# VectorE divides all 32 heads in one pass and rotates the keys of both batches in one pass

## The reference

```python
x = x + tanh(g_xattn[0]) * L0_xattn(layernorm(x), mask, ctx, Wq, Wk, Wv, Wo, gate)
x = x + tanh(g_ffn[0]) * L0_ffn(layernorm(x), wg, W, b)
x = x + tanh(g_xattn[1]) * L1_xattn(w, u, layernorm(x), ctx)
x = x + tanh(g_ffn[1]) * L1_ffn(layernorm(x), w_gate, w1, w2, w3)

# L0_xattn: 32 heads of 8 columns, rotary q and k
q = q * cos + rotate_half(q) * sin
k = k * cos + rotate_half(k) * sin
w = softmax(q @ k.T / sqrt(8) + mask)
attn = w @ v
a_scores = tanh(gate) * softmax(q @ a_k.T / sqrt(8))   # a_k, a_v from ctx, not rotated
attn = attn + a_scores @ a_v
return attn @ Wo
```

## Time and profile before

| | |
|---|---|
| median of 3 runs | 542.29 us (541.72 to 549.66) |
| the profiled execution | 543.49 us |
| its span in the trace | 541.6 us |
| TensorE busy | 476.9 us, 88% |
| TensorE weight loads | 355.0 us, 66% |
| VectorE busy | 392.6 us, 72% |
| ScalarE busy | 263.7 us, 49% |
| GpSimd busy | 169.7 us, 31% |
| mean granted clock of TensorE | 0.954 |
| loop over tiles | to about 300 us |

### The profile page before, as it was taken

How to read it: one execution, slowest core, us unless ns; L and a number is a source line. 1 busy time by engine, 2 the same in 40 slices (tenths; PEclk the granted TensorE clock), 3 DMA queues, 4 the chain that set the end, 5 groups by cost and what they waited for, 6 DMA issues and landing times. The chain is left out here.

```text
span 541.6 us, 10345 instructions
## 1 busy us (share of the span) xinstructions
PE 476.9 (88%) x3090; PEld 355.0 (66%) x3091; DVE 392.6 (72%) x1042; ACT 263.7 (49%) x562; POOL 169.7 (31%) x228
## 2 busy tenths in 40 slices
PE   4589999999989988988988859877889999999994
PEld 2458678667567576675776636545568788878782
DVE  4856878788897897888987777937676566556640
ACT  2546283374462662743731432511646666666651
POOL 4150204114113123141131143220345556555622
PEclk9888997999999999999998958988999999999997
DMA  7921304004004004022040179553657667767721
GB/s 239 278 42 21 62 3 79 5 23 79 5 21 79 15 10 77 24 38 45 21 80 6 39 301 422 201 159 128 229 146 232 206 204 230 249 208 195 232 27 21
DMA packets 24755, 63.38 MB, mean 117 GB/s; under 512 B 5161, under 2 KB 15281, under 8 KB 21777
## 3 DMA queue, kind: packets, MB, share of 16 engines
q1 hardware_dynamic: 19440, 56.38, 33.9%
q0 software_dynamic: 4416, 6.03, 6.1%
q10 hardware_dynamic: 864, 0.54, 0.3%
HBM read 48.79 MB, written 5.24 MB: 100 GB/s over the span
## 5 line engine op out<-in xcount | busy, mean ns | idle before, releaser
L1901 PE MATMUL bank_o<-w,hT 128*128 (+1 forms) x276 | 70.4, 398 | 1.1 <-DVE hT L1323 0.7
L1337 DVE TENSOR_TENSOR wl<-lw,wh 128x1024 fp32r<-128x1024 f32 (+1 forms) x54 | 60.9, 1129 | 0.3 <-ACT wh L621 0.3
L1901 PEld LDWEIGHTS bank_o<-w,hT 128*128 128x128 f32 (+1 forms) x276 | 50.4, 195 | 15.6 <-issue 10.0
L494 POOL TENSOR_SCALAR rstd<-mv 128x1 f32<-128x1 f32 x32 | 7.2, 225 | 168.4 <-DVE mv L956 168.4
L1028 DVE TENSOR_REDUCE mx<-bank_s 128x8 f32<-128x512 f32 x64 | 43.3, 686 | 14.7 <-PE bank_s L1645 14.2
L621 ACT ACTIVATE wh<-lw 128x1024 fp32r<-128x1024 f32 (+1 forms) x54 | 53.0, 981 | 0.0
L1643 PE MATMUL bank_s<-Kh,Qx 128*128 128x128 f32 x256 | 43.2, 293 | 4.6 <-DVE mx L1028 3.3
L1330 DVE TENSOR_TENSOR hh<-sg,bank_s 128x256 f32<-128x256 f32 x46 | 19.1, 418 | 35.9 <-ACT sg L849 26.8
L1643 PEld LDWEIGHTS bank_s<-Kh,Qx 128*128 128x128 f32 x256 | 37.1, 202 | 7.5 <-DVE mx L1028 4.0
L575 POOL DMA_INDIRECT out_x<-ys,idx_out x18 | 29.0, 1609 | 37.6 <-ACT ys L860 36.8
L662 ACT ACTIVATE Qx<-qs,CN 128x512 fp32r<-128x512 f32 x56 | 35.2, 710 | 5.5 <-DVE qs L1001 5.4
(11 more groups left out here) (346 smaller groups left out, 1157.3 us busy)
## 6 DMA issues: line engine op xcount, KB each, us to landing
lw<-in_w SPq DMA_DIRECT2D x18, 1408.0 KB, 6.5
Q<-Qx SPq DMA_DIRECT2D x16, 512.0 KB
up<-in_w SPq DMA_DIRECT2D x5, 1408.0 KB, 6.9
w<-in_w SPq DMA_DIRECT2D x4, 1536.0 KB, 11.8
Pt<-in_WT SPq DMA_DIRECT2D x1, 1024.0 KB, 11.8
X<-in_x SPq DMA_DIRECT2D x1, 896.0 KB, 8.3
CT<-in_ctxT SPq DMA_DIRECT2D x1, 896.0 KB, 8.7
out_x<-X SPq DMA_DIRECT2D x6, 128.0 KB, 1.7
```

The source lines that it names most:

```text
L1337: dve.tensor_tensor(wl[par][:, :, at:at + k], lw[par][:, :, at:at + k], wh[par][:, :, at:at + k].bitcast(F32), ALU.subtract).then_inc(w_lo, 1)
L1901: ins = pe.matmul(bo[:, 0:HID], hT[0:k, i, :], w2[0:k, bass.ts(e, 1), i, :].rearrange("p o n -> p (o n)"), start=(i == 0), stop=(i == IT - 1))
```

## The change

1. `heads` can do all 32 heads at once. In the loop it is called once per tile, where the first of its two calls stood, between the maxima of units 2 and 3; it waits for all four groups of `Oc` where the first call waited for three. In the last tile's tail the two calls stay.
2. `ao_in` counts one per tile instead of two; ScalarE's and TensorE's waits for it are changed to that.
3. `rotate_ks` rotates both batches' keys with the same four operations on operands twice as wide; it is called where the first `rotate_k` stood, ahead of the third norm's `ln_apply(2, u)`. The second call, behind it, is gone. The set-up of tile 0 still calls `rotate_k` twice.

```diff
@@ -689,7 +689,7 @@
                 if g == 0:
-                    after(act, ao_in, t - 1, 2, 2)
+                    after(act, ao_in, t - 1, 1, 1)
@@ -964,18 +964,23 @@
+            def both(ap):
+                return ap[:, :, :].rearrange("p b n -> p (b n)")
+
             def twice(ap):
-                return ap.rearrange("p (g o d) -> p g o d", g=G, o=1).to_broadcast([P, G, 2, HG * D])
+                n = ap.shape[-1] // (HG * D)
+                return ap.rearrange("p (g o d) -> p g o d", g=n, o=1).to_broadcast([P, n, 2, HG * D])
@@ -994,6 +999,15 @@
+            def rotate_ks(t):
+
+                after(dve, k_in, t, BT, BT)
+                rope(both(kw), C_COSK, C_SINK, both(kt1), both(kt2)).then_inc(rope_step, BT)
+                after(dve, rope_step, t, 1 + BT, 1 + BT)
+                after(dve, kT, t - 1, BT, BT)
+                dve.tensor_tensor(kr[:, :, :, :, :].rearrange("p b g o d -> p (b g) o d"), twice(both(kt1)), twice(both(kt2)),
+                                  ALU.add).then_inc(k_rot, BT)
@@ -1035,12 +1049,12 @@
-            def heads(t, part):
-
-                r = (slice(0, H - HG), slice(H - HG, H))[part]
+            def heads(t, part=None):
+
+                r = slice(0, H) if part is None else (slice(0, H - HG), slice(H - HG, H))[part]
                 n = r.stop - r.start
-                link = Chain(dve, heads_step, t, 6, 3 * part)
-                after(dve, o_in, t, G, (3, 4)[part])
+                link = Chain(dve, heads_step, t, 3, 3 if part == 1 else 0)
+                after(dve, o_in, t, G, 3 if part == 0 else G)
@@ -1395,10 +1409,8 @@
                 if prev:
-                    heads(u, 0)
+                    heads(u)
                 maxima(t, range(3, 4))
-                if prev:
-                    heads(u, 1)
                 maxima(t, range(4, 6))
@@ -1437,11 +1449,10 @@
                 if nxt:
-                    rotate_k(t + 1, 0)
+                    rotate_ks(t + 1)
                 if prev:
                     ln_apply(2, u)
                 if nxt:
-                    rotate_k(t + 1, 1)
                     mask_low(t + 1, 1 - par)
@@ -1709,7 +1720,7 @@
             def turn_heads(t, following, o=bc):
-                after(pe, ao_in, t, 2, 2)
+                after(pe, ao_in, t, 1, 1 if following else 2)
```

More of the change, by code:

```diff
@@ L965, in ln_apply @@
                                   ALU.subtract, ALU.mult).then_inc(ln_done[n], 1)
+            def both(ap):
+                return ap[:, :, :].rearrange("p b n -> p (b n)")
             def twice(ap):
-                return ap.rearrange("p (g o d) -> p g o d", g=G, o=1).to_broadcast([P, G, 2, HG * D])
+                n = ap.shape[-1] // (HG * D)
+                return ap.rearrange("p (g o d) -> p g o d", g=n, o=1).to_broadcast([P, n, 2, HG * D])
             def rope(src, cos, sin, t1, t2):
-                v = src.rearrange("p (h d) -> p h d", h=H)
+                m = src.shape[-1] // D
+                v = src.rearrange("p (h d) -> p h d", h=m)
                 def bc3(c, n):
-                    return c.rearrange("p (o d) -> p o d", o=1).to_broadcast([P, H, n])
-                a = t1.rearrange("p (h d) -> p h d", h=H)
-                z = t2.rearrange("p (h d) -> p h d", h=H)
+                    return c.rearrange("p (o d) -> p o d", o=1).to_broadcast([P, m, n])
+                a = t1.rearrange("p (h d) -> p h d", h=m)
+                z = t2.rearrange("p (h d) -> p h d", h=m)
                 h = D // 2
```

## The result

The changed kernel takes **551.91 us** (median of 4 runs, 550.89 to 562.09) against 542.0 for the kernel before on the same chip (4 runs): **1.018 times as long, 95% interval 1.0153 to 1.0206**. The forecast was 540.0 us in a range of 538.0 to 543.8, so the time lies on the other side and outside. The profiled execution took 552.45 us with a span of 550.6, which is 8.96 us more than the one of before. Ratios and means here leave out the executions that count as slow, more than 1.5% above the fastest of the same kernel, while medians, lowest and highest times hold all of them.

A forecast was written before the change was run, and what follows sets the result against it. The prediction saw TensorE and VectorE both nearly full, so waits between them decide. Heads gain 3.6 us and k's rotation costs 1.3, taking the median of 542.29 to 540.0 us, range 538.0 to 543.8.

The forecast's parts named there:

- Heads: One 1.94 us pass on VectorE brings ao earlier and removes TensorE's waits for it; gain 3.6 us over the loop.
- k: Merged rotation on VectorE takes 2.65 us; h3 starts 1.08 us later, decay scan 0.22 us later per tile, 1.3 us in all.
- Sum: Whole kernel: 3.6 us gained and 1.3 us lost, so 2.3 us less than the median of 542.29 us.
- A: All of VectorE's saving in both merged passes counts: 8.5 us, giving 533.8 us; chance 0.06.
- B: Wide heads pass runs over its price, so its gain is lost and h3's lateness stays: 543.6 us; chance 0.15.
- C: TensorE's 1.3 us idle ahead of h3 lowers its clock, costing 2 us of at most 3: 542.0 us; chance 0.13.
- fuller form: Clock falls between hn and the second norm cost 1.7 us each, six giving 550 us; chance 0.03 for over 545.
- The named sign of being wrong: In the profile after, a granted clock under 1.00 in most tiles would show the forecast wrong.
- The steps for k and for ao: Profile after: TensorE's ao waits near 0; k's merged sum 1.23 us, h3 wait 1.3 us, VectorE's kk wait 0.7 us.
- The period of 37.7 us: Profile after: the steady tile's period becomes 37.7 us instead of 38.0.
- The last phases shift as a whole: Phases behind the loop depend on its events, not on times, so they move together with it.

The follow-up runs named there:

- heads alone: Heads in one pass, k rotated batch by batch as in the kernel before; 545.6 us (median of 10), 1.0009 times before.
- k alone: Keys rotated in one pass, heads in two as in the kernel before, with ten counting instructions; 547.93 us (median of 10), 1.008 times before.
- head at 196: The changed kernel with ten semaphore counts ahead of VectorE's loop over tiles, work unchanged; 543.66 us (median of 10), 1.0005 times before.

## Why the prediction was wrong

**The step that failed** is the sentence in which I left out that the edit might do something else: "VectorE's program has 825 rows before and 761 after, and both merged forms stand in it". I used the lengths of the program to show that the edit is made, and gave the fact that it is shorter no consequence. The loading of instructions was thereby put at nothing without a reason: no term of the sum and no rival held it. What the runs show in its place: 15 instructions fewer ahead of the loop put its head across a loading edge, and the one jump back costs 4.72 + 2.11 us on VectorE, 5.9 us of the time at equal clock, and a stretch of low clock behind it.

**Heads.** Pass of 1.94 us: measured 1.94. Gain of 3.6 us, 0.6 in each of six tiles: 0.57 and 0.73 in two tiles with the clock at 1.00 between hn and h2, 3.1 (0.3) at equal clock with heads alone, and the waits for ao are gone. Right in mechanism and about right in size.

**k.** The four steps were to take 2.65 us; they take 203.89 - 201.17 = 2.72, with 0.21 us of idle time ahead of the wide sum, of 1.22 us (forecast 1.23). Kk is waited for by 0.63 us (forecast 0.72), and from the first step to the scan it is 4.07 us instead of the 3.79 of the earlier trace rows, 0.28 later where I had 0.22. TensorE's wait for h3 is 6.6 us in six, a mean of 1.1 and up to 1.6, as forecast (1.3). Its price of 0.22 us in a tile is 0.26 to 0.62 in the three tiles read above, so it was too low there. At equal clock the 1.3 us do not show: within their group of runs k alone is 0.6 us (0.5) over the kernel before, and both merges 0.5 us (0.4) under heads alone. The two views need not agree, since at equal clock a fall that a wait brings with it is not counted as the wait's.

**Sum.** -2.3 us was forecast, 0.38 in each of six tiles; without the stall the two tiles whose period is read above are 0.31 and 0.36 us shorter, and at equal clock it is -3.6 in all. In the median the kernel with its head at 196 is 1.0005 times the one before. There the clock takes back what the passes give.

**Rivals.** A (all of VectorE's time counts, 8.5 us) is refuted: no version is more than 3.6 us under the line. B (the heads' pass runs over its price) is refuted by 1.94 us. C (the clock falls) was given 0.13 at 542, and it happened: the mean clock is 0.943 against 0.951 at head 196, worth 2.9 us, where I had taken 2 of at most 3. That it comes from the wait for h3 alone is not shown. Its fuller form, falls in places where TensorE is last, got 0.03; the changed kernel shows two, one behind the stall, caused by loading and not by h3, and one at 216 us; with the head at 196 there is one at 132 us, of 1.5 us where I had 1.7. The named sign of being wrong, a granted clock under 1.00 in most tiles, was seen: from hn to hn the changed kernel has 0.91, 0.91, 0.92, 0.92 and 0.91, the kernel before 0.95, 0.91 and three times 1.00. The steps for k and for ao were seen. The period of 37.7 us was not, in the changed kernel: behind the tile of the stall, hn comes at 215.87 and 254.46, 38.6 us apart, with a window at 0.58 in between; with the head at 196 one is 37.66.

```profile
216.00:220.00 4.00, 3.55 (x13) 3.10 (x14) 3.43 (x8) 0.87 (x3) 0.54 (x3) 0.58 0.71 130
```

**"The last phases shift as a whole."** In the two profiled executions hn of tile 7 is 10.7 us later and the end 9.0, so they roughly do. With the head at 196 it is 1.2 us later and the end 0.8 us earlier, so the 2 us between them are as large as the gain that was forecast, and one pair of profiled executions can't show that gain from its ends.

## What to carry over

When an edit changes how many instructions an engine runs ahead of or inside a loop, count them: here a loop head that moved over a loading edge cost 6.8 us of VectorE's time at its one jump back, on code that had not changed. Test a surprising loss by adding a few harmless instructions ahead of the loop before looking for it in the work. Compare kernels at equal granted clock as well as by their medians, since a gain of half a per cent in waiting is easily less than what the clock does with the new pattern of waits.

## What the runs showed of the hardware

- VectorE's jump back over the edge near instruction 193 stalls it twice: 4.7 + 2.1 us, 4.9 + 2.5 and 4.5 + 1.8 in three kernels, the second time where the next block begins. It falls in 165 to 176 us, where the transfers of Q keep the DMA engines busy at 0.98; whether it would be shorter on idle queues was not tried.
- The instruction queue q14 carries 20 packets in the three kernels that stall and 15 to 17 in the eleven that do not.
- The time of one and the same program goes with its mean granted clock, 3.6 us for each 0.010, over 0.936 to 0.962 in 46 executions.
- Behind 6 us in which TensorE stood idle, its clock was at 0.50 for 4 us and at a mean of 0.68 for the next 4.
- A fall of the clock costs where TensorE is last: 9.21 us from hn to h2 against 7.74 at full clock. Behind the wait for h3 the period of the tile stayed 0.3 us shorter than before in spite of it.
